# A quarter of every third round's first group is fetched row by row, into two buffers in turn

## The chip, the cores and the metric

One core of one Trainium2 chip. The metric is the device time of the program in microseconds, lower is better. TensorE is PE, VectorE is DVE, ScalarE is ACT, GpSimd is POOL and SyncE is SP.

## The reference

One layer of a graph network with 12500 nodes and 200000 edges, 128 values each, float32:

```
h = relu(layernorm(x))
msg = relu(concat(h[src], h[dst], edge_attr) @ W1 + b1)      # W1: 384 x 128
aggr = segment_sum(msg, dst)
out = x + layernorm(aggr + h) * gamma + beta
```

The receivers dst are sorted, the senders src are not.

## The kernel before, in words

W1 is cut in three. The kernel first computes two tables in HBM, with one row for each node: table_a = h @ W_a and, a few blocks ahead of its use, table_b = h @ W_b + b1. Then it goes through the edges in groups of 512, which lie as 128 partitions by four quarters. Four groups are a round; there are 98 rounds and 391 groups. For the group u of round i:

- SP loads the edge rows and the receivers' numbers for two groups at once (`pair`), and for each group the 64 rows of table_b that its receivers fall into (`window`). The tiles hold one round. So a window is loaded only when the products of the same place in the round before have read it (s_pre), and a pair only when the transposes and the one-hot of the round before are done with it.
- PE transposes the edges (L756), ACT copies them out of PSUM (L991), DVE builds one-hot columns of the receivers (L1367), and PE multiplies both, edges by W_c and one-hot by the window (L769, L770), into one PSUM bank.
- POOL fetches the senders' rows of table_a with four indirect DMAs of 128 rows each (L613, `step`). Their buffers hold one round too: a step waits until the group one round earlier has been added (s_z).
- DVE adds gathered rows and products (L1387, `add_a`), ACT applies relu (L995), PE sums over equal receivers by a one-hot product (L781), and DVE adds the 64 sums into the aggregate in SBUF (L1408).

In each round one block of 128 nodes is finished and stored as well, and one block of table_b is made.

Two kinds of groups don't have all their rows from POOL. In the last round of each six the fourth group comes whole from a table of early rows, which SP loads with one DMA (`load_early`, L497). And in that same round the last quarter of the first group is fetched by hand: the row numbers lie in SBUF as byte offsets (hand_picks), SP and ACT load them into registers (L363, one TENSOR_LOAD for each batch) and issue one DMA of 512 bytes for each row (L508, L1027). Of the 128 rows SP fetches 64, in eight batches of eight, two in each of rounds 1 to 4 of the six (counted from 0), and ACT 64, in batches of four, one in each group of rounds 1 to 4. The first batch waits until the buffer has been read. DVE then adds three quarters from POOL's rows and the last from hand_rows (L1390, L1394).

Each engine goes through its own program in the order in which it is written: within a round that is the order of its `round_`, and semaphores alone tie the engines together. SP, ACT and POOL have a loop whose body is six rounds, called a turn below. SP's rows stand behind the window of the second and of the fourth group of a round.

Of the kernel before, what the change touches and what calls it, by code (L numbers as in the profile page):

```python
# [31 lines left out]
P = 128  # L32
H = 128
EPS = 1e-5
SUB = 4
# [12 lines left out]
PERIOD = 6  # L48
BATCH = 8
HAND_K = SUB - 1  # L50
ACT_ROWS = 64
# [7 lines left out]
def build(nc, x, src, dst, edge_attr, w1, b1, gamma, beta, out):  # L59
# [30 lines left out]
    assert HANDS * PERIOD == ROUNDS - 2 and EARLY % PERIOD == 0 and SP_ROWS % BATCH == 0  # L90
# [7 lines left out]
    with ctx:  # L98
# [69 lines left out]
        hand_rows = sb("hand_rows", [P, 1, H])  # L168
# [122 lines left out]
        s_hand_rows = [sem("s_hand_rows")]  # L291
# [89 lines left out]
        def _(sp):  # L381
# [71 lines left out]
            with sp.If(crooked < 1):  # L453
# [57 lines left out]
                def round_(i, t=None, par=None, j=None):  # L511
# [10 lines left out]
                def rounds(s):  # L522
                    for j in range(EARLY):
                        n = j // PERIOD
                        round_(s * EARLY + j, s * (EARLY // PERIOD) + n, 0, j % PERIOD)
# [10 lines left out]
                with sp.Fori(1, EARLY_GROUPS) as s:  # L536
                    rounds(s)
                round_(ROUNDS - 2)
# [31 lines left out]
        def _(pool):  # L570
# [35 lines left out]
            with pool.If(crooked < 1):  # L606
# [10 lines left out]

                def rounds(s):

                    for n in range(EARLY // PERIOD):  # L620
# [3 lines left out]
                        for u in range(UNROLL if n < EARLY // PERIOD - 1 else UNROLL - 1):  # L624
                            step(s * EARLY + (n + 1) * PERIOD - 1, u, HAND_K if u == 0 else SUB)

                for i in range(EARLY):
                    hand = i % PERIOD == PERIOD - 1
                    for u in range(UNROLL if i < EARLY - 1 else UNROLL - 1):
                        step(i, u, HAND_K if hand and u == 0 else SUB)  # L630
# [242 lines left out]
        def _(act):  # L873
# [111 lines left out]
            with act.If(crooked < 1):  # L985
# [33 lines left out]
                def fetch(t, par, slot):  # L1019

                    if slot == UNROLL and past(t, 1):
                        act.wait_ge(s_z, ((t - 1) * PERIOD + PERIOD - 1) * UNROLL + 1)
                        act.sem_inc(s_gate_act, 1)
                    first = SP_ROWS + sum(ACT_SLOTS[:slot])
                    numbers = numbers_of(mybir.EngineType.Activation, t, first, ACT_SLOTS[slot])
                    for n in range(ACT_SLOTS[slot]):
                        act.dma_start(hand_row(first + n, par), row_at(numbers[n])).then_inc(s_hand_rows[par], 16)  # L1027

                def round_(i, groups=UNROLL, early=False, early_before=False, t=None, par=None, j=None):
                    last = groups < UNROLL  # L1030
                    for u in range(groups):
                        if not (last and u == groups - 1):
                            columns(*after(i, u, 1))
                        if t is not None and j * UNROLL + u < len(ACT_SLOTS) and ACT_SLOTS[j * UNROLL + u]:
                            fetch(t, par, j * UNROLL + u)
# [21 lines left out]

                ACT_SLOTS = [0] * UNROLL + [4] * (ACT_ROWS // 4)
                assert sum(ACT_SLOTS) == ACT_ROWS and len(ACT_SLOTS) < PERIOD * UNROLL

                def rounds(t, early):
                    for j in range(PERIOD):
                        round_(t * PERIOD + j, early=early, early_before=early and (past(t, 1) or j > 0), t=t, par=0, j=j)
# [4 lines left out]
                with act.Fori(1, EARLY_ROWS // PERIOD) as t:  # L1068
                    rounds(t, True)
                t = EARLY_ROWS // PERIOD  # L1070
                for j in range(PERIOD):
                    i = t * PERIOD + j
                    round_(i, early=i < EARLY_ROWS, early_before=i <= EARLY_ROWS, t=t, par=0, j=j)
                with act.Fori(t + 1, HANDS) as t:
                    rounds(t, False)
# [42 lines left out]
        def _(dve):  # L1118
# [232 lines left out]
            with dve.If(crooked < 1):  # L1351
# [21 lines left out]
                def add_a(i, u, turn, loaded, handed):  # L1373
# [6 lines left out]
                    else:  # L1380
                        for k in range(HAND_K if handed is not None else SUB):
                            own = u == UNROLL - 1 or (u == 0 and k == HAND_K)
                            dve.wait_ge(s_a_rows[u][k], (turn if own else i + 1) * 16)  # L1383
# [222 lines left out]
```

## Time and profile before

| | us |
|---|---|
| median of 3 runs | 1952.32 (1952.24 to 1952.49) |
| span of the profiled execution | 1949.5 |
| PE busy | 1548.5 |
| POOL busy | 1463.9 |
| DVE busy | 1256.9 |
| ACT busy | 659.4 |

Shares on the page are of the span. What an engine's sequencer does, such as issuing DMAs, loading registers and waiting for semaphores, doesn't count as busy; it is shown with a q behind the engine's name (SPq, ACTq). SP has no busy time at all on the page, since all that it does is of that kind. "issue" as what ended an idle time means that the engine waited for nothing that the profile shows.

### The profile page before, as it was taken

The page shows a single profiled execution, that of the slowest core. Times are in us where ns is not written, and L with a number is a line of the kernel's source. Part 1 is how long each engine was busy: PE and PEld are TensorE (multiplying, and loading weights), DVE is VectorE, ACT ScalarE, POOL GpSimd, SP SyncE. Part 2 cuts the span into 40 slices and gives each one's busy share as a digit, 9 for nine tenths or more (in the row PEclk, how much of TensorE's full clock was granted, in tenths as well). Part 3 has the DMA queues.
Part 4 walks back from the last instruction along what each step waited for, and adds up shares of the span by engine and source line. Part 5 has one row for each costly group of instructions (what it writes and reads, how often), then busy time and mean ns, then how long its engine had stood idle before and what let it go on. Part 6 is the DMA issues. An engine that isn't in the chain of part 4 may idle for free.

```text
span 1949.5 us, 52908 instructions
## 1 busy us (share of the span) xinstructions
PE 1548.5 (79%) x11881; PEld 1483.7 (76%) x11881; DVE 1256.9 (64%) x3454; ACT 659.4 (34%) x1507; POOL 1463.9 (75%) x1559
## 2 busy tenths in 40 slices
PE   5688788778878787877787788787788888877887
PEld 5678788777777777877777787777777877777786
DVE  7656666667666666666666676666566665656665
ACT  5533333333333333333333333333323232322323
POOL 7777777777777777777777777777777777777776
PEclk9888888989889998998989998999898888888988
DMA  9755656556565655656565565656556565555554
GB/s 261 204 143 144 167 143 166 152 156 166 144 169 145 164 152 155 163 147 169 149 160 153 155 166 144 168 140 168 147 154 163 138 164 148 155 148 153 163 145 106
DMA packets 229468, 306.84 MB, mean 157 GB/s; under 512 B 46461, under 2 KB 141157, under 8 KB 229317
## 3 DMA queue, kind: packets, MB, share of 16 engines
q1 hardware_dynamic: 151858, 192.55, 34.4%
q0 software_dynamic: 49536, 101.55, 21.4%
q10 hardware_dynamic: 27922, 11.43, 2.7%
q14 instruction: 143, 1.16, 0.2%
q8 instruction: 9, 0.15, 0.0%
HBM read 281.72 MB, written 23.64 MB: 157 GB/s over the span
## 4 chain that ended last, share of the span: by engine, by line
issue 22%; DMA 22%; POOL 20%; PE 13%; DVE 10%; DVEq 8%; ACT 2%; ACTq 2%; POOLq 1%; SPq 0%
DMA a_rows<-table_a,picks 20%; POOL a_rows L613 19%; DVEq L1398 5%; DVE onehot_cols L1367 3%; PE ps_pre L769 3%; PE ps_pre L770 3%; PE ps_sum L781 2%; DVE msg L1387 2%; PE ps_edge L756 2%; PE ps_fin L781 1%; DVE aggr L1408 1%; ACTq L1027 1%; DMA table_a<-a_out 1%; DVEq L1383 1%; PE ps_sum L788 1%
## 5 line engine op out<-in xcount | busy, mean ns | idle before, releaser
L613 POOL DMA_INDIRECT a_rows<-table_a,picks x1484 | 1401.8, 945 | 452.4 <-issue 400.3
L769 PE MATMUL ps_pre<-w_c,edge_cols 128*128 128x128 f32 x3128 | 671.5, 300 | 29.5 <-issue 29.2
L770 PE MATMUL ps_pre<-b_win,onehot_cols 128*128 128x128 f32 x3128 | 663.2, 297 | 0.0
L995 ACT ACTIVATE msg<-msg 128x512 f32<-128x512 f32 x390 | 245.7, 630 | 951.9 <-DVE msg L1387 893.1
L769 PEld LDWEIGHTS ps_pre<-w_c,edge_cols 128*128 128x128 f32 x3128 | 537.1, 215 | 38.6 <-issue 37.0
L1387 DVE TENSOR_TENSOR msg<-ps_pre,a_rows 128x512 f32<-128x512 f32 x374 | 257.0, 687 | 433.8 <-DMA a_rows<-table_a,picks 339.4
L770 PEld LDWEIGHTS ps_pre<-b_win,onehot_cols 128*128 128x128 f32 x3128 | 534.7, 214 | 0.0
L1367 DVE SCALAR_TENSOR_TENSOR onehot_cols<-space,base_all,ps_hot 64x512 f32<-64x512 int32 x391 | 438.3, 1121 | 0.6 <-DMA space<-in_dst 0.6
L781 PE MATMUL ps_sum<-onehot,msg 128*128 128x64 f32 x1560 | 214.6, 283 | 105.2 <-ACT e_rows L1013 71.3
L781 PEld LDWEIGHTS ps_sum<-onehot,msg 128*128 128x128 f32 x1560 | 200.5, 201 | 123.4 <-ACT e_rows L1013 82.2
L991 ACT ACTIVATE edge_cols<-ps_edge 128x512 f32<-128x512 f32 x391 | 228.4, 584 | 136.8 <-PE ps_edge L756 115.7
L756 PE MATMUL ps_edge<-ident,edges 128*128 128x128 f32 x1564 | 264.9, 297 | 8.4 <-DMA edges<-in_edge_attr 8.4
L781 PE MATMUL ps_fin<-onehot,msg 128*128 128x64 f32 x1560 | 212.2, 283 | 5.6 <-ACT msg L995 5.6
L781 PEld LDWEIGHTS ps_fin<-onehot,msg 128*128 128x128 f32 x1560 | 205.2, 205 | 7.3 <-DVE aggr L1408 6.9
L756 PEld LDWEIGHTS ps_edge<-ident,edges 128*128 128x128 f32 x1564 | 201.6, 162 | 10.5 <-DMA edges<-in_edge_attr 5.9
L1355 DVE TENSOR_TENSOR onehot<-dst_f,ps_hot 128x256 f32<-128x256 f32 x391 | 161.0, 412 | 41.8 <-issue 34.5
L788 PE MATMUL ps_sum<-ident,e_norm 128*128 128x128 f32 x64 | 24.8, 388 | 120.8 <-DVE e_norm L1426 120.8
L788 PEld LDWEIGHTS ps_sum<-ident,e_norm 128*128 128x128 f32 x64 | 10.0, 156 | 129.8 <-DVE e_norm L1426 129.8
L737 PE MATMUL ps_fin<-ident,staged 128*128 128x128 f32 x97 | 29.6, 305 | 79.3 <-DVE aggr L1408 76.0
L1408 DVE TENSOR_TENSOR aggr<-ps_fin,aggr 128x64 f32 x195 | 43.9, 225 | 72.0 <-issue 44.6
L1408 DVE TENSOR_TENSOR aggr<-ps_sum,aggr 128x64 f32 x196 | 43.8, 224 | 65.8 <-PE ps_sum L781 37.9
L737 PEld LDWEIGHTS ps_fin<-ident,staged 128*128 128x128 f32 x97 | 14.4, 149 | 85.4 <-DVE aggr L1408 83.8
(137 smaller groups left out, 1073.8 us busy)
## 6 DMA issues: line engine op xcount, KB each, us to landing
edges<-in_edge_attr SPq DMA_DIRECT2D x195, 512.0 KB
space<-in_dst SPq DMA_DIRECT2D x195, 256.0 KB
a_rows<-table_a,picks POOLq DMA_INDIRECT x1484
hand_rows<-table_a SPq DMA_DIRECT2D x1024, 0.5 KB
hand_rows<-table_a ACTq DMA_DIRECT2D x1024, 0.5 KB
b_win<-table_b SPq DMA_DIRECT2D x391, 32.0 KB
table_b<-b_rows ACTq DMA_DIRECT2D x96, 64.0 KB
out<-out_rows SPq DMA_DIRECT2D x96, 64.0 KB
```

The costliest lines, as they stand in the source:

```text
L613: pool.indirect_dma_start(a_rows[:, u, k, :], None, table_a[:, :], bass.IndirectOffsetOnAxis(ap=picks[:, u, k:k + 1], axis=0),).then_inc(s ...
L756: mm = pe.transpose(ps_edge[u % 2][:, k * P:(k + 1) * P], edges[:, u, k * H:(k + 1) * H], ident[:, :])
L769: pe.matmul(to, edge_cols[:, u % 2, k * P:(k + 1) * P], w_c[:, :], start=True, stop=False)
L770: mm = pe.matmul(to, onehot_cols[:, u % 2, k * P:(k + 1) * P], b_win[:, u, :], start=False, stop=True)
L781: mm = pe.matmul(ps_sums[u % 2], msg[:, u % 2, k, :], onehot[:, u, k, 0:WIN], start=(k == 0), stop=(k == SUB - 1))
L991: act.activation(edge_cols[:, u % 2, :], ps_edge[u % 2][:, :], ACT.Copy).then_inc(s_edge_cols, 1)
L995: act.activation(msg[:, u % 2, :, :], msg[:, u % 2, :, :], ACT.Relu).then_inc(s_msg, 1)
L1355: dve.tensor_tensor(onehot[:, u, :, 0:WIN], dst_f[:, bass.ds(i * UNROLL + u, 1), :].rearrange("p o k -> p (o k)").unsqueeze(2) .to_broadca ...
L1367: dve.scalar_tensor_tensor(out=onehot_cols[0:WIN, u % 2, :].rearrange("w (k p) -> w k p", k=SUB), in0=dst_win[:, u, :].rearrange("w (p k) ...
L1387: dve.tensor_tensor(msg[:, u % 2, :, :].rearrange("p k f -> p (k f)"), ps_pre[u % 2][:, :], a_rows[:, u, :, :].rearrange("p k f -> p (k f) ...
L1398: return dve.value_load(base_i[0:1, bass.ds(g, 1)], min_val=0, max_val=N - 1)
L1408: dve.tensor_tensor(at, ps_sums[u % 2], at, ALU.add).then_inc(s_added, 1)
```

## The change

A quarter is fetched by hand in every third round in place of every sixth, so 32 times in place of 16. POOL leaves that gather out in the first group of rounds 2 and 5 of each turn. hand_rows has two buffers, used in turn, with a semaphore each. Of the 128 rows SP now fetches 80 and ACT 48. The rows for one use are spread over the three rounds before it: SP has six batches of 13 or 14 rows, behind the windows of the second and the fourth group as before, and ACT has four rows in each of twelve groups. The very first set is fetched in two rounds (SP in four batches of 20, ACT six rows in each group), and the last round of the last turn has no batch. DVE's loops are cut at every third round, and its waits count the gathers of each buffer anew. The core of the diff:

```diff
-PERIOD = 6
-BATCH = 8
+PERIOD = 3
-ACT_ROWS = 64
+ACT_ROWS = 48
...
-        hand_rows = sb("hand_rows", [P, 1, H])
+        hand_rows = sb("hand_rows", [P, 2, H])
...
+        def hand_slots(s, j):
+
+            t = s * 2 + (0 if j < 2 else 1 if j < EARLY - 1 else 2)
+            third = j + 1 if j < 2 else j - 2 if j < EARLY - 1 else 0
+            return t, (j + 1) // PERIOD % 2, third
+
+        def hands_used(t):
+
+            return ((t - 2) * PERIOD + PERIOD - 1) * UNROLL + 1
...
-                def fetch(t, par, batch):
-
-                    if batch == 0 and past(t, 1):
-                        sp.wait_ge(s_z, ((t - 1) * PERIOD + PERIOD - 1) * UNROLL + 1)
+                def fetch(t, par, first, n):
+
+                    if first == 0 and past(t, 2):
+                        sp.wait_ge(s_z, hands_used(t))
                         sp.sem_inc(s_gate_sp, 1)
-                    numbers = numbers_of(mybir.EngineType.SP, t, batch * BATCH, BATCH)
-                    for n in range(BATCH):
-                        sp.dma_start(hand_row(batch * BATCH + n, par), row_at(numbers[n])
-                                     ).then_inc(s_hand_rows[par], 16)
+                    numbers = numbers_of(mybir.EngineType.SP, t, first, n)
+                    for p in range(n):
+                        sp.dma_start(hand_row(first + p, par), row_at(numbers[p])).then_inc(s_hand_rows[par], 16)
...
-                        if t is not None and (j, u) in SP_SLOTS:
-                            fetch(t, par, SP_SLOTS.index((j, u)))
+                        if hands is not None and u % PAIR == 1:
+                            t, par, parts = hands
+                            fetch(t, par, *parts[u // PAIR])
...
-                SP_SLOTS = [(j, u) for j in range(1, PERIOD - 1) for u in (1, 3)]
-                assert len(SP_SLOTS) * BATCH == SP_ROWS
+                def parts(number):
+
+                    ends = [SP_ROWS * n // number for n in range(number + 1)]
+                    return [(first, end - first) for first, end in zip(ends, ends[1:])]
+
+                SP_PARTS, SP_FIRST = parts(2 * PERIOD), parts(4)
...
+                def hand_round(i, groups):
+                    for u in range(groups):
+                        step(i, u, HAND_K if u == 0 else SUB)
+
                 def rounds(s):
 
-                    for n in range(EARLY // PERIOD):
+                    for n in range(2):
                         with pool.Fori(n * PERIOD, (n + 1) * PERIOD - 1) as j:
                             for u in range(UNROLL):
                                 step(s * EARLY + j, u)
-                        for u in range(UNROLL if n < EARLY // PERIOD - 1 else UNROLL - 1):
-                            step(s * EARLY + (n + 1) * PERIOD - 1, u, HAND_K if u == 0 else SUB)
+                        hand_round(s * EARLY + (n + 1) * PERIOD - 1, UNROLL - n)
...
-                ACT_SLOTS = [0] * UNROLL + [4] * (ACT_ROWS // 4)
+                SLOT, FIRST_SLOT = ACT_ROWS // (PERIOD * UNROLL), ACT_ROWS // (2 * UNROLL)
...
-                        dve.wait_ge(s_hand_rows[0], handed * (P * 16))
-                        dve.tensor_tensor(msg[:, u % 2, HAND_K, :], ps_pre[u % 2][:, HAND_K * H:], hand_rows[:, 0, :],
+                        dve.wait_ge(s_hand_rows[par], handed * (P * 16))
+                        dve.tensor_tensor(msg[:, u % 2, HAND_K, :], ps_pre[u % 2][:, HAND_K * H:], hand_rows[:, par, :],
                                           ALU.add).then_inc(s_z, 1)
```

SP's program in the first round of a turn, from the window of the second group to the pair of the third and fourth, before:

```order
L484 REGISTER_ALU
L486 ISA
L486 DMA b_win<-table_b 64x128
L461 ISA
L461 DMA edges<-in_edge_attr 128x2x512
L462 REGISTER_ALU
L462 DMA space<-in_dst 64x1024
```

And now (L495 is the window, L470 and L471 are the pair, L372 is the load of row numbers, L517 the rows):

```order
L493 REGISTER_ALU
L495 ISA
L495 DMA b_win<-table_b 64x128
L372 ISA
L372 TENSOR_LOAD hand_picks
L517 DMA hand_rows<-table_a 1x512 x14
L470 ISA
L470 DMA edges<-in_edge_attr 128x2x512
L471 REGISTER_ALU
L471 DMA space<-in_dst 64x1024
```

A register load and fourteen rows stand between window and pair in a round that had none.

SP's program at the end of a turn, from the window of the fourth group of the sixth round to the jump back, before (L490 is the output store, L497 the load of early rows):

```order
L484 REGISTER_ALU
L486 ISA
L486 DMA b_win<-table_b 64x128
L490 ISA
L490 DMA out<-out_rows 128x128
L495 ISA
L497 ISA
L497 DMA a_rows<-table_early 128x4x128
L536 REGISTER_ALU
L536 COMPARE_AND_BRANCH
```

And now (L499 is the output store, L506 the load of early rows):

```order
L495 ISA
L495 DMA b_win<-table_b 64x128
L372 REGISTER_ALU
L372 TENSOR_LOAD hand_picks
L517 DMA hand_rows<-table_a 1x512 x13
L499 ISA
L499 DMA out<-out_rows 128x128
L504 ISA
L506 ISA
L506 DMA a_rows<-table_early 128x4x128
L554 REGISTER_ALU
L554 COMPARE_AND_BRANCH
```

A batch of thirteen rows stands ahead of the output store, the load of early rows and the jump back.

## Rows read from the trace of the kernel before

**Rows 1.** The page: span, busy time, granted clock by slice, the gather

```profile
span 1949.5 us, 52908 instructions
...
PE 1548.5 (79%) x11881; PEld 1483.7 (76%) x11881; DVE 1256.9 (64%) x3454; ACT 659.4 (34%) x1507; POOL 1463.9 (75%) x1559
...
PEclk9888888989889998998989998999898888888988
...
L613 POOL DMA_INDIRECT a_rows<-table_a,picks x1484 | 1401.8, 945 | 452.4 <-issue 400.3
```

**Rows 2.** Waits of POOL, whole run: line, us in total, times, longest

```profile
POOL a_rows L613 <- issue: 400.3, 1313, 0.3
```

**Rows 3.** L613, 191.8 to 1787.2 us: count, ns min/median/max, first and last

```profile
L613 POOL DMA_INDIRECT a_rows<-table_a,picks x1277: 940/944/1071, 192.0 to 1786.3; - x183
```

**Rows 4.** Waits of DVE, whole run

```profile
DVE msg L1387 <- DMA a_rows<-table_a,picks: 339.4, 154, 5.4
```

**Rows 5.** Waits of SP's queue, 191.8 to 1787.2 us

```profile
SPq L485 <- PE ps_pre L770: 297.5, 89, 8.8
SPq L459 <- DVE onehot_cols L1367: 123.9, 60, 6.7
SPq L490 <- DVE out_rows L1340: 75.5, 30, 5.3
```

**Rows 6.** Timeline of SP: start us, us, line, operation, tiles, count

```profile
1027.92 0.41 SPq L461 DMA_DIRECT2D edges<-in_edge_attr  x1
...
1031.55 2.56 SPq L508 DMA_DIRECT2D hand_rows<-table_a  x8
...
1042.36 2.50 SPq L508 DMA_DIRECT2D hand_rows<-table_a  x8
...
1100.81 0.38 SPq L497 DMA_DIRECT2D a_rows<-table_early  x1
1105.91 0.39 SPq L461 DMA_DIRECT2D edges<-in_edge_attr  x1
```

**Rows 7.** Instructions of L508, whole run

```profile
L508 SPq DMA_DIRECT2D hand_rows<-table_a x1024: 218/225/328, 93.3 to 1878.0; - x171
```

**Rows 8.** Register loads, whole run by tile, then two single ones

```profile
L363 ACTq TENSOR_LOAD <-hand_picks x256: 331/492/696, 110.6 to 1890.0; - x128
L363 SPq TENSOR_LOAD <-hand_picks x128: 525/761/977, 92.6 to 1874.6; - x128
...
L474 SPq TENSOR_LOAD <-base_i x98: 303/569/683, 73.3 to 1914.6; - x98
...
L363 SPq TENSOR_LOAD <-hand_picks x1: 542/542/542, 1014.1 to 1014.1; - x1
...
L363 SPq TENSOR_LOAD <-hand_picks x1: 910/910/910, 1022.8 to 1022.8; - x1
```

**Rows 9.** Timeline of PE: a turned group, products after it, later ones

```profile
1036.46 0.68 PE L756 MATMUL ps_edge<-ident,edges 128*128 128x128 f32 x4
1036.95 0.63 PE L769 MATMUL ps_pre<-w_c,edge_cols 128*128 128x128 f32 x2
...
1041.65 0.39 PE L769 MATMUL ps_pre<-w_c,edge_cols 128*128 128x128 f32 x2
```

**Rows 10.** DMA issue: KB each, median us to landing

```profile
w_c<-in_L_gnn_W SPq DMA_DIRECT2D x1, 64.0 KB, 5.1
```

**Rows 11.** ACT: its longest wait, then four rows in its timeline

```profile
ACT msg L995 <- DVE msg L1387: 893.1, 355, 13.1
...
1090.66 1.45 ACTq L1027 DMA_DIRECT2D hand_rows<-table_a  x4
```

**Rows 12.** Instructions of L1394, whole run

```profile
L1394 DVE TENSOR_TENSOR msg<-ps_pre,hand_rows x16: 268/280/281, 193.1 to 1897.3; 128x128 f32<-128x128 f32 x16
```

**Rows 13.** Waits of SP's queue, 73.3 to 191.8 us

```profile
SPq L485 <- PE ps_pre L770: 30.7, 7, 6.6
SPq L459 <- DVE onehot_cols L1367: 17.8, 5, 8.5
```

More of the change, by code:

```diff
@@ L1017, in store_early, with fetch, round_ @@
                     act.dma_start(table_early[bass.ds(r * P, P), :], e_rows[:, :]).then_inc(s_e_stored, 16)
-                def fetch(t, par, slot):
-                    if slot == UNROLL and past(t, 1):
-                        act.wait_ge(s_z, ((t - 1) * PERIOD + PERIOD - 1) * UNROLL + 1)
+                def fetch(t, par, first, n):
+                    if first == 0 and past(t, 2):
+                        act.wait_ge(s_z, hands_used(t))
                         act.sem_inc(s_gate_act, 1)
[L1024 to L1029, printed above, removed]
+                    numbers = numbers_of(mybir.EngineType.Activation, t, SP_ROWS + first, n)
+                    for p in range(n):
+                        act.dma_start(hand_row(SP_ROWS + first + p, par), row_at(numbers[p])
+                                      ).then_inc(s_hand_rows[par], 16)
+                def round_(i, groups=UNROLL, early=False, early_before=False, hands=None):
                     last = groups < UNROLL
@@ L1033, in round_ @@
                             columns(*after(i, u, 1))
-                        if t is not None and j * UNROLL + u < len(ACT_SLOTS) and ACT_SLOTS[j * UNROLL + u]:
-                            fetch(t, par, j * UNROLL + u)
+                        if hands is not None:
+                            t, par, first, n = hands
+                            fetch(t, par, first + u * n, n)
                         if u == 3 and past(i, 2):
@@ L1067, in _ @@
                 rounds(0, True)
[L1068 to L1075, printed above, removed]
+                with act.Fori(1, EARLY_ROWS // EARLY) as s:
+                    rounds(s, True)
+                half = EARLY_ROWS // EARLY
+                for j in range(EARLY):
+                    i = half * EARLY + j
+                    round_(i, early=i < EARLY_ROWS, early_before=i <= EARLY_ROWS, hands=hands_of(half, j))
+                with act.Fori(half + 1, EARLY_GROUPS - 1) as s:
+                    rounds(s, False)
+                rounds(EARLY_GROUPS - 1, False)
                 round_(ROUNDS - 2)
@@ L1431, in clear, with round_ @@
                     dve.tensor_copy(aggr[:, bass.ds((j + AHEAD) * P, P)], ps_zero.to_broadcast([P, P]))
-                def round_(i, turn, groups=UNROLL, early=False, loaded=None):
+                def round_(i, turn, groups=UNROLL, early=False, loaded=None, handed=None, par=None):
                     last = groups < UNROLL
@@ L1480, in _ @@
                 dve.wait_ge(s_early_raw, EARLY_ROWS * 16)
-                def rounds(s, early):
-                    with dve.Fori(0, EARLY - 1) as j:
-                        round_(s * EARLY + j, s * (EARLY - 1) + j + 1, early=early)
-                    round_(s * EARLY + EARLY - 1, None, early=early, loaded=s + 1)
-                for i in range(3):
-                    round_(i, i + 1, early=True)
-                with dve.Fori(3, EARLY - 1) as i:
-                    round_(i, i + 1, early=True)
@@ L1490, in _, with turns @@
-                round_(EARLY - 1, None, early=True, loaded=1)
-                with dve.Fori(1, EARLY_ROWS // EARLY) as s:
-                    rounds(s, True)
-                half = EARLY_ROWS // EARLY
-                with dve.Fori(EARLY_ROWS - EARLY_REST, EARLY_ROWS) as i:
-                    round_(i, i - half + 1, early=True)
-                with dve.Fori(EARLY_ROWS, half * EARLY + EARLY - 1) as i:
-                    round_(i, i - half + 1)
-                round_(half * EARLY + EARLY - 1, None, loaded=half + 1)
+                def turns(s, j):
+                    return s * (EARLY - 2) + j + (1 if isinstance(j, int) and j < PERIOD else 0), s * (EARLY - 1) + j + 1
@@ new lines, in _ @@
+                for j in range(PERIOD - 1):
+                    round_(j, turns(0, j), early=True)
+                first_hand(0, True)
+                with dve.Fori(PERIOD, EARLY - 1) as j:
+                    round_(j, turns(0, j), early=True)
+                second_hand(0, True)
+                half = EARLY_ROWS // EARLY
+                with dve.Fori(1, half) as s:
+                    rounds(s, True)
+                for j in range(PERIOD - 1):
+                    round_(half * EARLY + j, turns(half, j), early=True)
@@ L1499, in _ @@
+                first_hand(half, True)
+                for j in range(PERIOD, EARLY - 1):
+                    round_(half * EARLY + j, turns(half, j), early=j < EARLY_REST)
+                second_hand(half, False)
                 with dve.Fori(half + 1, EARLY_GROUPS) as s:
                     rounds(s, False)
-                round_(ROUNDS - 2, ROUNDS - 1 - EARLY_GROUPS)
-                round_(ROUNDS - 1, ROUNDS - EARLY_GROUPS, LEFT)
+                round_(ROUNDS - 2, turns(EARLY_GROUPS, 0))
```

61 lines of the change are left out of this document (44 added, 17 removed).

## The prediction

> **What bounds the kernel now.** I read the page first, then who waits for whom, engine by engine, and then single lines. No compute engine is full: the page gives PE 79%, POOL 75%, DVE 64% of the span [rows 1]. But POOL's 75% is the part that the profile counts as busy. Its gather takes 945 ns, 1484 times, and all idle time before gathers is 452.4 us [rows 1], 0.305 us each; in 1313 cases nobody is named for it, and the longest of these is 0.3 us [rows 2]. So a gather costs 945 ns plus 0.3 us whatever the others do, and POOL never stands still for anyone. Take the middle of the run, 191.8 to 1787.2 us, which is 14 turns of the six-round loops (from the start of one turn in SP's stream to that of another): 1277 gathers in 1595.4 us are 1.249 us each [rows 3]. One turn of six rounds takes 1595.4 / 14 = 113.96 us, and 91 gathers of 1.249 us are 113.7 us. The other side of it stands with DVE: its longest wait is for the gathered rows, 339.4 us in 154 waits [rows 4]. POOL bounds the kernel before, and each gather taken from it is worth 1.25 us, for as long as nobody else needs the time.
>
> SP is the next stream to look at, because the change loads it and the page does not show it as an engine at all. In the same 14 turns SP waited 297.5 us for products (to reload a window), 123.9 us for the one-hot (to reload edges) and 75.5 us for output rows: 496.9 us, or 35.5 us a turn [rows 5]. The other 113.96 - 35.5 = 78.5 us of each turn are SP's own instructions, with nothing to wait for. Part of it is the jump back: from the early-table load at 1100.81 to the next edge load at 1105.91 are 5.1 us in which no wait is named [rows 6].
>
> **What the change removes.** Sixteen more groups have their fourth quarter fetched by hand, so POOL has 1484 - 16 = 1468 gathers, 90 a turn instead of 91: 112.4 us a turn. If POOL stayed the bound the kernel would gain 16 x 1.249 = 20.0 us. That is also the most it can gain. POOL's wait for the fetch buffers does not exist (hand rows have their own tile), and two buffers give each set three rounds to be filled and three until it is overwritten, so I cost the gate on the buffer at nothing: the set before last was used three rounds earlier. If that cover failed, the wait would stand on SP's stream, which is priced below.
>
> **What it adds on SP.** Rows a turn go from 64 to 2 x 80 = 160, so 96 more. Eight rows take 2.56 us from first to last, 2.50 at another place [rows 6]; a DMA instruction of 225 ns [rows 7] and the setting up between two of them, 0.32 us all told. 96 x 0.32 = 30.7 us.
>
> Each batch begins with a load of its numbers into registers. Before, 8 loads a turn took 525 to 977 ns, median 761; single ones are 542 ns for the first batch of a round and 910 ns for the second [rows 8]. After there are 12 a turn, each of 13 or 14 numbers instead of 8, and no row shows one of that size. Lower bound: a load costs the same whatever it holds, mean 0.73 us, so 12 x 0.73 - 8 x 0.73 = 2.9 us. Upper bound: in proportion to the numbers, 0.73 x 13.3 / 8 = 1.21 us, 12 x 1.21 - 5.8 = 8.7 us. Between them is the growth from four to eight numbers: SP's loads of four bases take 303 to 683 ns and those of eight 525 to 977 [rows 8], so some 0.055 to 0.08 us a number, which makes 13.3 numbers 0.8 us where the load is quick and 1.3 us where it is slow, 1.06 in the mean: 12 x 1.06 - 5.8 = 6.9 us. I take this one, since both rows it is drawn from are of this engine. The Trainium skill says two things here. DMA: Bandwidth & Descriptors, Latency and other measured facts, puts the floor of a tensor_load at about 600 ns: as a flat price that is 12 x 0.6 = 7.2 us, 1.4 more than now, and on that side the change would come out faster (the second case below). Runtime: NRT & Kernel Launch, Instruction fetch mechanics, has about 200 ns a register, which would be 2.7 us for a load of 13 and a clearly slower kernel, but by that rule eight numbers would take 1.6 us, and the trace has 0.54 and 0.91; the measurement decides, and neither rule is in the sum.
>
> Small things on SP: rounds 0 and 5 of each turn had no rows, and now have them. Loads of bases right after a batch are the slow kind, so two more a turn become slow, 2 x 0.28 = 0.5 us; batch starts and a longer loop body, some 0.6 us (bounds 0 and 1.5).
>
> Sum for SP a turn: 78.5 + 30.7 + 6.9 + 0.5 + 0.6 = 117.2 us, bounds 78.5 + 30.7 + 2.9 = 112.1 and 78.5 + 30.7 + 8.7 + 0.5 + 1.5 = 119.9. POOL would need 112.4, and the turn took 113.96. So the 35.5 us in which SP waited are used up, SP becomes the bound, and a turn takes 3.2 us more than before, not 1.25 less. What queues behind the rows on SP are the edge pairs and the windows: a window can't be loaded before the products of a round earlier have read the old one, so SP can't work ahead by more than about a round, and its lead (the pair issued at 1027.92 is first turned by PE at 1036.46 [rows 6, 9], 8.5 us, of which a landing must be kept, some 4 to 5 us, a little under the 5.1 us that the page gives for a load early in the run [rows 10]) is worth some 4 or 5 us once, not each turn.
>
> At the end of round 5 the batch now stands ahead of the load of early rows. It delays that load by 13 rows and a register load, 5.4 us. DVE needs the tile only after products that the window just before has released, and SP then jumps back and loads edges that PE turns ahead of those products, 5 us later still; so the early rows aren't the last to come. Nothing for it, and at worst 16 x 2 = 32 us if they are.
>
> **On ACT and DVE.** ACT's rows go from 64 to 96 a turn: 8 more batches of 0.49 us for the load and 1.45 us for four rows [rows 8, 11], 16 us a turn, in rounds 0 and 5, where there were none. ACT waits 893.1 us for DVE's sum [rows 11], and the new batches stand just in that wait, as those in rounds 1 to 4 already do while POOL sets the pace. Nothing, and if half a microsecond showed in each it would be 4 us a turn, still beside SP's slack. DVE's sum falls in two parts in 16 more groups, 280 ns for the second part [rows 12] less what the first part saves, under 3 us in all, beside its 339.4 us of waiting. PE has the same work; its granted clock is 0.8 to 0.9 of full in every slice [rows 1], and I leave that.
>
> **The total.** The profiled execution is 1949.5 us long, the runs' median 1952.3, so 2.8 us lie around the span. 14 turns x 3.2 = +45. The first turn (from 73.3 to 191.8, 118.5 us, of which SP waited 48.5 in its two longest waits [rows 8, 13]) has 123 more rows, 39 us, and 9 us more for loads: it fits, with +2. The last turn (1787.2 to 1896.9) took 109.7 us and has no batch in its last round, so SP has room again: -3. The lead that is given up once: -4. Sum: 1952.3 + 45 + 2 - 3 - 4 = 1992.3. I say 1992.
>
> **Rivals.** (1) Loads don't grow with what they hold: SP needs 112.1 to 113.3 us a turn, just at POOL's 112.4, and the kernel gains 1.25 to 0.7 us a turn: 1932 to 1942, faster. It decides from a mean load under about 0.8 us (12 x 0.8 - 5.8 = 3.8 us, a turn of 113). For it: there is a large fixed part in each load. Against it: eight take longer than four at both levels [rows 8], and even here every wait of SP must vanish, though it waits for three different engines. (2) In between, SP needs 113.5 to 114.4, a turn as long as now: 1948 to 1956. (3) SP is full and still has to wait at times, since its lead is gone and the landing of an edge pair now stands in the open before PE: pair, landing, turn, products, next window. From window to window that is about 7.7 us of issuing, 1.5 us for the pair, 5 us to land and 3 to 4 us on PE, some 17 to 18 us, against 19.5 us for SP's own round; with PE at the lower clock, where two products take 0.63 us in place of 0.39 [rows 9], it comes near. At 2 to 4 us a turn: 2025 to 2055. For it: 35.5 us of waits came from this loop. (4) That the change doesn't do what it says: the order of instructions has the batches where the text puts them, so no.
>
> **The chances.** SP full by itself 0.64, rival 3 0.11, rival 2 0.08, rival 1 0.17. Slower by over 0.2% (about what a measurement can tell from no change): 0.64 + 0.11 = 0.75; same 0.08; faster 0.17. The range: 112.1 a turn gives 1932, 119.9 gives 1952.3 + 14 x 5.9 - 5 = 2030. I leave out the best end and most of rival 3, so 1941 to 2028; the likeliest case alone has 1970 to 2024.
>
> **What would show it.** SP's waits for products, one-hot and output rows fall from 496.9 us to under 60 in the middle turns. POOL's gathers remain 945 ns, but the idle time before some of them is now a wait for DVE's sum, 4 to 5 us a turn. DVE waits for products or windows, no longer for gathered rows. Loads of 13 or 14 numbers take about 0.8 and 1.3 us. A turn takes 117 us. I am wrong if POOL's gathers still follow each other by 1.25 us, if the loads take 0.54 and 0.91, or if rows cost other than 0.32 us.

## The result, and the profile after

| | before | after |
|---|---|---|
| median, us | 1952.37 (1952.24 to 1952.49) | 2247.12 (2245.63 to 2249.88) |
| ratio | | 1.151, 95% interval 1.150 to 1.153 |
| span of the profiled execution | 1949.5 | 2243.8 |
| granted PE clock, mean | 0.899 | 0.851 |

The forecast was slower, 1992 us, range 1941 to 2028. The direction came true, the size not: 295 us lost and not 40.

The first question is whether POOL or SP sets the pace now. From the page after, against [rows 1]:

```profile
PE 1613.6 (72%) x11881; PEld 1555.3 (69%) x11881; DVE 1270.1 (57%) x3470; ACT 671.4 (30%) x1507; POOL 1448.1 (65%) x1543
...
SPq 68%; issue 19%; PE 5%; POOL 3%; DMA 3%; DVE 0%; ACTq 0%; ACT 0%; DVEq 0%; POOLq 0%
SPq L517 27%; SPq L372 19%; SPq L495 8%; SPq L471 4%; SPq L470 4%; POOL aggr L607 3%; SPq L483 2%; DMA edges<-in_edge_attr 2%; SPq L499 2%; PE ps_pre L793 1%; PE ps_pre L794 1%; PE ps_edge L780 1%; POOL a_rows L632 1%; DMA a_rows<-table_a,picks 1%; PE ps_sum L805 1%
...
L632 POOL DMA_INDIRECT a_rows<-table_a,picks x1468 | 1385.9, 944 | 762.3 <-issue 447.0
```

POOL has its 16 gathers fewer, of 944 ns each (945 before), but its idle time before them rose from 452.4 to 762.3 us. The chain that ended last is SP's for 68% of the span: the rows (L517), the loads of their numbers (L372), the windows (L495). PE's granted clock is lower than before, but PE has only 5% of that chain.

Fourteen middle turns lie between 203.0 and 2081.9 us (a turn begins with SP's load of bases in its first round). They take 134.21 us each; before it was 113.96. Asked for waits of SP's queue in that stretch, where [rows 5] had 496.9 us, the profile names none. DVE and PE wait for what SP loads, in the same stretch (who waited for whom; us in total, times, longest):

```profile
DVE onehot_cols L1402 <- DMA space<-in_dst: 366.1, 112, 9.4
```

```profile
PE ps_edge L780 <- DMA edges<-in_edge_attr: 413.2, 130, 10.3
```

So SP is full. Its rows cost what they did, against [rows 7]; its loads don't. First the rows, then all loads of hand_picks by SP, in the middle turns, and then four single ones: the third and the fourth batch of one set, and the first and the second of the next (count: ns min/median/max, first and last start in us):

```profile
L517 SPq DMA_DIRECT2D hand_rows<-table_a x2240: 218/225/316, 209.9 to 2080.1; - x187
```

```profile
L372 SPq TENSOR_LOAD <-hand_picks x168: 994/2905/3442, 206.9 to 2072.9; - x168
...
L372 SPq TENSOR_LOAD <-hand_picks x1: 2977/2977/2977, 1010.4 to 1010.4; - x1
...
L372 SPq TENSOR_LOAD <-hand_picks x1: 1393/1393/1393, 1021.1 to 1021.1; - x1
...
L372 SPq TENSOR_LOAD <-hand_picks x1: 1012/1012/1012, 1054.9 to 1054.9; - x1
...
L372 SPq TENSOR_LOAD <-hand_picks x1: 3145/3145/3145, 1063.8 to 1063.8; - x1
```

Loads of 13 or 14 numbers take either 1.0 to 1.4 us or 2.7 to 3.4, while [rows 8] had 0.53 to 0.98 for eight. The load at 1054.9 is the first batch of a set and starts at number 0; the one at 1063.8 has as many numbers and starts at 13. The fourth batch of a set, from number 40 (here at 1021.1), is the other quick one. 0 and 40 are multiples of four; 13, 26, 53 and 66 are not. The loads of a turn sum to 29.4 us. The four loads of the very first set point the same way: they hold 20 numbers each, start at 0, 20, 40 and 60, and take 1.2 to 1.65 us.

### The profile page after: what moved, and what is told of

Its sections match the earlier page's. It is cut to its first block, busy times and chain, and to the rows that moved or that the text cites. A ratio compares the mean times of both kernels' runs of the same rounds, so it can differ in the third digit from the quotient of the medians.

```text
span 2243.8 us, 57022 instructions
## 1 busy us (share of the span) xinstructions
PE 1613.6 (72%) x11881; PEld 1555.3 (69%) x11881; DVE 1270.1 (57%) x3470; ACT 671.4 (30%) x1507; POOL 1448.1 (65%) x1543
## 4 chain that ended last, share of the span: by engine, by line
SPq 68%; issue 19%; PE 5%; POOL 3%; DMA 3%; DVE 0%; ACTq 0%; ACT 0%; DVEq 0%; POOLq 0%
SPq L517 27%; SPq L372 19%; SPq L495 8%; SPq L471 4%; SPq L470 4%; POOL aggr L607 3%; SPq L483 2%; DMA edges<-in_edge_attr 2%; SPq L499 2%; PE ps_pre L793 1%; PE ps_pre L794 1%; PE ps_edge L780 1%; POOL a_rows L632 1%; DMA a_rows<-table_a,picks 1%; PE ps_sum L805 1%
## 5 line engine op out<-in xcount | busy, mean ns | idle before, releaser
L632 POOL DMA_INDIRECT a_rows<-table_a,picks x1468 | 1385.9, 944 | 762.3 <-issue 447.0
L793 PE MATMUL ps_pre<-w_c,edge_cols 128*128 128x128 f32 x3128 | 704.6, 313 | 10.6 <-issue 9.3
L794 PE MATMUL ps_pre<-b_win,onehot_cols 128*128 128x128 f32 x3128 | 697.1, 310 | 0.0
L780 PE MATMUL ps_edge<-ident,edges 128*128 128x128 f32 x1564 | 286.2, 313 | 453.2 <-DMA edges<-in_edge_attr 452.6
L793 PEld LDWEIGHTS ps_pre<-w_c,edge_cols 128*128 128x128 f32 x3128 | 572.9, 228 | 13.3 <-issue 11.9
L794 PEld LDWEIGHTS ps_pre<-b_win,onehot_cols 128*128 128x128 f32 x3128 | 568.8, 227 | 0.0
L805 PE MATMUL ps_sum<-onehot,msg 128*128 128x64 f32 x1560 | 230.7, 297 | 81.5 <-ACT e_rows L1037 60.0
L805 PEld LDWEIGHTS ps_sum<-onehot,msg 128*128 128x128 f32 x1560 | 218.3, 216 | 98.8 <-ACT e_rows L1037 70.9
L607 POOL DMA_INDIRECT aggr<-in_x,early_picks x64 | 60.6, 947 | 22.4 <-issue 18.9
L997 ACT ACTIVATE o_dev<-o_moments,eps 128x1 f32<-128x1 f32 x96 | 28.3, 294 | 155.2 <-issue 154.2
L1227 DVE CAST picks<-src_f 128x4 int32 (+1 forms) x391 | 70.6, 181 | 0.0
L812 PE MATMUL ps_sum<-ident,e_norm 128*128 128x128 f32 x64 | 21.2, 331 | 48.4 <-DVE e_norm L1461 47.7
```

Source lines behind the costliest of these rows:

```text
L632: pool.indirect_dma_start(a_rows[:, u, k, :], None, table_a[:, :], bass.IndirectOffsetOnAxis(ap=picks[:, u, k:k + 1], axis=0),).then_inc(s ...
L780: mm = pe.transpose(ps_edge[u % 2][:, k * P:(k + 1) * P], edges[:, u, k * H:(k + 1) * H], ident[:, :])
L793: pe.matmul(to, edge_cols[:, u % 2, k * P:(k + 1) * P], w_c[:, :], start=True, stop=False)
L794: mm = pe.matmul(to, onehot_cols[:, u % 2, k * P:(k + 1) * P], b_win[:, u, :], start=False, stop=True)
L805: mm = pe.matmul(ps_sums[u % 2], msg[:, u % 2, k, :], onehot[:, u, k, 0:WIN], start=(k == 0), stop=(k == SUB - 1))
```

## The experiments

In the table "turn" is the mean of the fourteen middle turns, "waits" SP's named waits in them, and "own" the difference: SP's instructions with nothing to wait for. POOL's 90 gathers are 112.4 us a turn. Each ratio is taken against runs of the kernel before made beside it, whose medians were 1951.1 to 1954.9 us. Names such as 64 and 48 give SP's rows and ACT's rows of a set.

| kernel | us | ratio to before, interval | turn | waits | own |
|---|---|---|---|---|---|
| before | 1952.4 | | 114.0 | 35.5 | 78.5 |
| after | 2247.1 | 1.151, 1.150 to 1.153 | 134.2 | 0 | 134.2 |
| starts by four | 2013.1 | 1.031, 1.030 to 1.033 | 118.4 | 1.0 | 117.4 |
| padded | 2050.7 | 1.050, 1.049 to 1.052 | 121.1 | 0.7 | 120.4 |
| no loads | 1933.2 | 0.991, 0.989 to 0.992 | 112.4 | 12.1 | 100.3 |
| before, shifted | 1951.0 | 1.000, 0.999 to 1.001 | 114.0 | 27.3 | 86.7 |
| 64 and 64 | 1989.7 | 1.020, 1.017 to 1.023 | 116.6 | 11.5 | 105.1 |
| 72 and 56 | 1951.1 | 1.000, 0.999 to 1.001 | 113.9 | 2.4 | 111.5 |
| 64 and 48 | 1933.6 | 0.991, 0.990 to 0.993 | 112.3 | 7.1 | 105.2 |
| 68 and 60 | 1945.5 | 0.997, 0.995 to 0.998 | 113.6 | 4.8 | 108.8 |
| 72 and 56, merged | 1934.4 | 0.992, 0.990 to 0.993 | 112.4 | 3.7 | 108.7 |
| 80 and 48, merged | 1979.9 | 1.013, 1.012 to 1.015 | 116.0 | 1.5 | 114.5 |

**Loads by themselves, first try.** 96 loads at the end of SP's program, their results unused.

```diff
+                for n in LOAD_SIZES:
+                    for first in LOAD_STARTS:
+                        numbers_of(mybir.EngineType.SP, 0, first, n)
```

> The kernel before, with 96 register loads added at the very end of SP's program, ahead of its last two waits: sizes 1, 2, 4, 8, 12, 13, 14 and 16 numbers, each from twelve starts (0, 1, 2, 3, 4, 8, 16, 13, 26, 40, 53, 66). Their numbers aren't used. Theory A (alignment): a load that starts at a multiple of four numbers (16 bytes) takes 0.3 to 1.0 us, growing by some 0.05 us a number; one that starts elsewhere takes about 0.2 us for each number, so 13 numbers from 13, 26, 53 and 66 take 2.6 to 2.9 us and from 0 and 40 at most 1.0 us. Theory B (count): the start makes no difference, and what costs is a size above eight or one that is no multiple of four: 13 and 14 take 2.6 us or more from every start, 12 and 16 do not. Theory C (neighbours): the slow loads of the changed kernel come from the row DMAs and other traffic around them; alone all sizes stay under 1.2 us. The time is longer than before by what the loads take beyond the wait for the last stores, under 150 us; it tells nothing else.

1954.9 us, and the trace has no load more than before (128 of hand_picks): what nobody uses was left out of the built program. It tells nothing of the theories.

**Starts by four.**

```diff
-                SP_PARTS, SP_FIRST = parts(2 * PERIOD), parts(4)
+                SP_PARTS, SP_FIRST = [(0, 12), (12, 12), (24, 16), (40, 12), (52, 12), (64, 16)], parts(4)
```

> The changed kernel, with SP's six batches of 12, 12, 16, 12, 12 and 16 rows in place of 13 or 14, so that each starts at a multiple of four numbers; as many rows and loads. Theory A: the twelve loads of a turn take 0.8 to 1.5 us each, some 13 us a turn in place of 29.3; SP stays full, the turn falls from 134.3 to 117 to 119 us and the time to 1985 to 2020. Theory B: batches of twelve and sixteen aren't slow either if the fault is a size that is no multiple of four, with the same time; if it is a size above eight, the loads stay near 2.9 us and the time near 2247. Theory C: no change, 2247.

2013.1 us, from 2247.1 with as many rows and loads. The loads:

```profile
L372 SPq TENSOR_LOAD <-hand_picks x190: 752/1136/1652, 76.3 to 1936.9; - x190
```

Theory A, and its turn of 117 to 119 us. Theory C (neighbours) falls; B in its form "a size above eight" falls too. That twelve and sixteen are multiples of four leaves the other form of B.

**Padded.** The batches stay at 13 and 14 rows; each one's numbers get a place of their own.

```diff
+            for m in range(6):
+                a, z = SP_ROWS * m // 6, SP_ROWS * (m + 1) // 6
+                dve.tensor_scalar(hand_picks[:, P + 16 * m:P + 16 * m + z - a], hand_ids[:, a:z, HAND_K],
+                                  float(ROW_BYTES), None, ALU.mult)
...
-                    numbers = numbers_of(mybir.EngineType.SP, t, first, n)
+                    at = first if (first, n) in SP_FIRST else P + 16 * [p[0] for p in SP_PARTS].index(first)
+                    numbers = numbers_of(mybir.EngineType.SP, t, at, n)
```

> The changed kernel with its batches of 13 and 14 rows as they are, but the numbers of each batch copied to a place of its own in hand_picks that starts at a multiple of sixteen numbers (six small DVE copies more, once). Theory A: loads of 13 and 14 take 1.0 us, or 1.4 behind another batch, some 14.5 us a turn in place of 29.3, a turn of 119 us, 2000 to 2025 in all. Theory B (size): no change, 2247. Theory C: no change, 2247.

2050.7 us, 26 over the upper end. The loads took 15.4 us a turn where 14.5 had been worked out, and 0.7 us of waits a turn, which the expectation had left out, stand on top of a full SP:

```profile
L372 SPq TENSOR_LOAD <-hand_picks x190: 981/1330/1693, 77.0 to 1977.4; - x190
```

The same sizes at aligned starts take 1.3 us in place of 2.9. So the start decides nearly all, and a size that is no multiple of four costs some 0.2 us more.

**No loads.** SP's rows come from fixed addresses.

```diff
-                    numbers = numbers_of(mybir.EngineType.SP, t, first, n)
+                    numbers = [(first + p) * ROW_BYTES for p in range(n)]
```

> The changed kernel without SP's register loads: SP fetches rows of fixed addresses, as many and in the same places (the rows it fetches are not those of the senders; ACT's are). If SP's own instructions are the bound, 134.3 - 29.3 = 105 us a turn, or a little less since an address needs no register, are below POOL's 112.4, and the kernel is bound by POOL as before: 1930 to 1940, the full 20 us gained. If instead the 512-byte DMAs themselves, their queue or their landings hold up the pairs and windows, the time stays above 2100.

1933.2 us: the whole worth of the sixteen gathers, 19 of 20 us. The 160 small DMAs a turn hold up nothing; what they cost is SP's time to issue them. (Here they read the same 80 rows again and again. Further down, kernels that fetch the senders' rows, 128 and 144 a turn on SP, reach the same time.) "Own" fell by more than the loads' 29.4 us, to 100.3: a fixed address needs no register, and the 160 moves of 29 ns that stand ahead of the DMAs in the changed kernel, 4.6 us a turn, are gone from the trace.

**Loads by themselves, used.**

```diff
+                for n in LOAD_SIZES:
+                    for first in LOAD_STARTS:
+                        numbers = numbers_of(mybir.EngineType.SP, 0, first, n)
+                        for m in range(n):
+                            ...
+                            sp.dma_start(hand_row(extra % P, 0), row_at(numbers[m])).then_inc(s_more_rows, 16)
+                            extra += 1
```

> The kernel before, with 56 register loads added at the end of SP's program, each followed by one 512-byte row DMA for every number that it loaded, so that the loads can't be dropped as unused: sizes 1, 4, 6, 8, 12, 13 and 16, each from starts 0, 1, 2, 4, 8, 13, 26 and 40. The rows go to a buffer that nobody reads any more. Theory A (alignment): from 0, 4, 8 and 40 a load takes 0.3 to 0.6 us for 4 numbers, 0.9 to 1.4 for 8 to 16; from 1, 2, 13 and 26 about 0.2 us for each number, 0.9 for 4, 1.8 for 8, 2.9 for 13, 3.5 for 16. Theory B (size): no difference between starts. The difference of 13 from 12 at the same start tells whether a rest that is no multiple of four costs extra: 0.2 us more under A.

The loads, by number of values and start, in ns:

```
        start   0      1      2      4      8     13     26     40
 1 number     280    487    484    506    506    499    502    507
 4            529   1136   1124    570    564   1131   1132    564
 6           1005   1528   1527    984    978   1558   1521    985
 8            796   1928   1925    787    783   1835   1921    789
12           1010   2732   2726   1005   1008   2727   2727   1008
13           1243   2928   2928   1237   1234   2923   2928   1230
16           1238   3532   3528   1242   1232   3531   3527   1232
```

Two pairs of them as the trace has them, for 8 and 13 numbers; the quick one starts at 4 and 8, the slow one at 2 and 13:

```profile
L366 SPq TENSOR_LOAD <-hand_picks x1: 787/787/787, 2015.5 to 2015.5; - x1
...
L366 SPq TENSOR_LOAD <-hand_picks x1: 1925/1925/1925, 2010.9 to 2010.9; - x1
...
L366 SPq TENSOR_LOAD <-hand_picks x1: 1234/1234/1234, 2108.0 to 2108.0; - x1
...
L366 SPq TENSOR_LOAD <-hand_picks x1: 2923/2923/2923, 2113.9 to 2113.9; - x1
```

Off a multiple of four, four numbers and more take 0.33 us and 0.2 us for each number. On it, 0.056 us a number in whole fours, and more for a rest: six take 0.99, more than eight. A single number takes 0.5 us from either kind of start; the 280 ns are the first load of all, with no row DMAs ahead of it. The rest is as theory A has it. The time of this run, 2198 us, is that of the added rows at its end and tells nothing else.

**Before, with shifted borders.** It asks whether slow loads hurt as such, or only where SP has no room.

```diff
-                    numbers = numbers_of(mybir.EngineType.SP, t, batch * BATCH, BATCH)
+                    first = batch * BATCH - (2 if batch else 0)
+                    size = BATCH + (2 if batch == 7 else -2 if batch == 0 else 0)
+                    numbers = numbers_of(mybir.EngineType.SP, t, first, size)
```

> The kernel before, with the borders of SP's batches moved by two: 6, then six times 8, then 10 rows, so that seven of eight loads a turn start two past a multiple of four. As many rows and loads. Theory A: those loads take 1.7 to 2.5 us in place of 0.54 and 0.91, 8 to 11 us more a turn on SP, which has 35.5 us of waiting: the loads get slow, SP's waits fall to about 25 us a turn and the time stays within 0.2% of 1952. If slow loads cost in themselves, by holding the pairs and windows late, it is slower by 5 us or more.

```profile
L363 SPq TENSOR_LOAD <-hand_picks x128: 733/1858/2535, 92.1 to 1874.8; - x128
```

Loads of 1.86 us in place of 0.76, 8.2 us more a turn of SP's own time, its waits down from 35.5 to 27.3, and the time equal to 0.1%. The waits were room, and these 8.2 us of it could be used up at no cost.

**64 and 64.** With starts right, how many rows can SP take?

```diff
-ACT_ROWS = 48
+ACT_ROWS = 64
+SP_SIZES, SP_FIRST_SIZES = [12, 8, 12, 12, 8, 12], [16, 16, 16, 16]
+ACT_SIZES, ACT_FIRST_SIZES = [4, 4, 8, 4, 4, 8, 4, 4, 8, 4, 4, 8], [8, 8, 8, 8, 8, 8, 8, 8]
```

> The changed kernel with SP fetching 64 rows in batches of 12, 8, 12, 12, 8, 12 and ACT 64 in 4, 4, 8 repeated; all batches start at a multiple of four numbers. SP's own instructions: 117.6 us a turn in the run with starts by four, less 32 rows of 0.32 us and a little less for loads, 106 to 107, under POOL's 112.4. ACT has eight groups a turn with eight rows, 1.5 us longer there. If SP's instruction time alone was the bound, POOL is it again and the time is 1930 to 1940. If the long ACT batches delay relu and so the sums, 1945 to 1970.

Both miss: 1989.7 us. SP's own time is 105.1, a little under the 106 to 107 worked out, and it waits 11.5 us a turn; POOL waits too, for up to 7.3 us. In the chain that ended last, ACT's queue stands where SP's was, and the timeline of ACT shows how (start, us, engine, line, operation; what ended the idle time before it in brackets):

```profile
PE 32%; issue 18%; ACTq 18%; POOL 8%; DMA 7%; DVE 6%; SPq 4%; ACT 3%; DVEq 3%; POOLq 0%
```

```profile
812.45 0.58 ACT L1016 ACTIVATE edge_cols<-ps_edge 128x512 f32<-128x512 f32 x1
812.95 2.94 ACTq L1051 DMA_DIRECT2D hand_rows<-table_a  x8
816.02 0.28 ACT L1038 ACTIVATE e_rows<-ps_sum 128x128 f32<-128x128 f32 x1 [3.00 <-issue]
816.20 0.62 ACT L1020 ACTIVATE msg<-msg 128x512 f32<-128x512 f32 x1
```

In each of the first 64 rounds ACT also copies a block for the early table out of PSUM, first as columns and then as rows, in the fourth and in the second group, each behind that group's batch. Above, the copy of early rows and then relu stand behind eight rows for 3.00 us. PE waits 103.1 us for those rows and 105.9 for the early columns in this run; with fours alone (64 and 48, below) it is 74.8 and 47.7. Turns with early rows (the first eleven) take 119.3 us on SP. In the later ones ACT has as many rows in the same batches, and POOL's gathers follow each other by 1.249 us again, 360 steps in 449.7 us (window 1400 to 1850 us), so neither ACT's rows nor their batches of eight hold anything up there:

```profile
L633 POOL DMA_INDIRECT a_rows<-table_a,picks x361: 940/944/1057, 1399.7 to 1849.4; - x181
```

I had cost ACT's batches at nothing, and batches of eight ahead of early rows and columns are not.

**72 and 56.**

```diff
+ACT_ROWS = 56
+SP_SIZES, SP_FIRST_SIZES = [12, 12, 12, 12, 12, 12], [20, 16, 20, 16]
+ACT_SIZES, ACT_FIRST_SIZES = [4, 4, 8, 4, 4, 4, 4, 4, 8, 4, 4, 4], [8, 8, 8, 4, 8, 8, 8, 4]
```

> The same with SP fetching 72 rows in six batches of 12, and ACT 56, in 4, 4, 8, 4, 4, 4 repeated. SP's own instructions 117.6 - 16 x 0.32 = 112.5 us a turn, less a little for loads, say 112, as much as POOL's 112.4. Two full streams with waits between them: 1935 to 1960, slower than the run with 64 and 64 if SP's remaining room is what counts, equal to it if a few us of room are enough.

1951.1 us, inside the range and no change to before, with SP nearly full: 111.5 own, 2.4 waiting. Both readings are wrong: it is neither slower than 64 and 64 nor equal to it but faster, although 64 and 64 has more room on SP.

**64 and 48.** As 64 and 64, with all of ACT's batches in the loop four rows; 16 rows of each set aren't fetched.

```diff
+ACT_ROWS = 48
+ACT_SIZES, ACT_FIRST_SIZES = [4, 4, 4, 4, 4, 4, 4, 4, 4, 4, 4, 4], [8, 4, 8, 4, 8, 4, 8, 4]
...
+            dve.memset(hand_rows[:, :, :], 0.0)
...
-                        dve.wait_ge(s_hand_rows[par], handed * (P * 16))
+                        dve.wait_ge(s_hand_rows[par], handed * ((P - 16) * 16))
```

> As the run with 64 rows on SP and 64 on ACT, but ACT fetches 48 in fours, as in the changed kernel, so that 16 rows of each set are not fetched at all and their places keep zeros (the messages of those edges lack the sender's part). It asks why 64 and 64 took 1990 us, 119 to 121 us a turn, with 14 us of waiting on SP. Theory: ACT's batches of eight stand between its copy of the edges and its relu and hold up PE's sums; with fours alone nothing is in POOL's way, SP needs 105 us a turn, and the time is 1930 to 1938. Rival: SP needs more room than its own instruction time leaves, since its lead is short; then it stays at 1960 to 1990.

1933.6 us, with 105.2 us on SP, as in 64 and 64. ACT's part made the difference of 56 us. This run changes two things in it, batches of four and sixteen rows a set fewer. The later turns of 64 and 64 speak against the rows as such, but they have no early copies; in the turns that have them the two are not separated.

**68 and 60.**

```diff
+SP_SIZES, SP_FIRST_SIZES = [12, 12, 12, 12, 12, 8], [20, 16, 16, 16]
+ACT_SIZES, ACT_FIRST_SIZES = [4, 4, 8, 4, 4, 4, 8, 4, 4, 4, 8, 4], [8, 8, 8, 4, 8, 8, 8, 8]
```

> The changed kernel with 68 rows on SP in batches of 12, 12, 12, 12, 12, 8 and 60 on ACT, which has eight rows only in the third group of a round and four elsewhere, where ACT has no copy of early columns or rows behind it. SP needs 111.9 - 8 x 0.32 = 109.3 us a turn. If the long ACT batches cost wherever they stand, 1955 to 1975, between 1951 (two a set) and 1990 (four a set). If they cost only in the second and fourth group, where early rows and columns wait behind them, 1932 to 1948, faster than before.

1945.5 us, inside the second case: against none (64 and 48), three long batches a set, all in the third group, and four more rows on SP cost 12 us. Four long batches a set, one at each of the four places in a round, had cost 56. The number and the place of the long batches changed together, and SP's rows with them, so how the cost is shared is not settled.

**Merged loads.** One load for the two batches of a round, with 72 and 56 rows:

```diff
+                    elif first % 24 == 0:
+                        both = numbers_of(mybir.EngineType.SP, t, first, 2 * n)
+                        kept[:] = both[n:]
+                        numbers = both[:n]
+                    else:
+                        numbers = kept
```

> The changed kernel with 72 rows on SP and 56 on ACT as in the run with that split, but SP loads the 24 numbers of a round at once and issues twelve rows behind the second window and twelve behind the fourth: 6 loads a turn of 24 numbers, 1.7 to 2.0 us each by the growth of aligned loads (0.06 us a number), in place of 12 of some 1.1. SP needs 2 to 3 us a turn less, 109 to 110. If SP is what holds the 72 and 56 split at 114.5 us a turn in its first two thirds, the time falls from 1951 to 1938 to 1948; if ACT's long batches hold it, it stays at 1951.

```profile
L374 SPq TENSOR_LOAD <-hand_picks x97: 1204/1487/1638, 76.7 to 1843.4; - x97
```

1934.4 us, 4 under the expected range and better than both kernels (0.992 of before, 0.861 of after). 24 numbers take 1.49 us, less than I had; SP's own time falls by 2.8 us to 108.7. So SP's instructions held 72 and 56, and not ACT's two long batches a set, which stand in the third group of one round and the first of another. POOL's gathers have no idle time over 0.9 us, near the 0.3 of before the change:

```profile
POOL a_rows L642 <- DVE picks L1234: 47.6, 154, 0.9
```

**80 and 48, merged.** The same on the changed kernel's own split, loads of 28, 24 and 28 numbers from 0, 28 and 52.

```diff
-                SP_PARTS, SP_FIRST = parts(2 * PERIOD), parts(4)
+                SP_PARTS, SP_FIRST = [(0, 14), (14, 14), (28, 12), (40, 12), (52, 14), (66, 14)], parts(4)
...
-                    numbers = numbers_of(mybir.EngineType.SP, t, first, n)
+                    elif SP_PARTS.index((first, n)) % 2 == 0:
+                        both = numbers_of(mybir.EngineType.SP, t, first, 2 * n)
+                        kept[:] = both[n:]
+                        numbers = both[:n]
```

> The changed kernel with its split of 80 and 48 rows and ACT's batches as they are; SP loads the 28, 24 and 28 numbers of a round at once, from starts 0, 28 and 52, and issues half of the rows behind the second window and half behind the fourth. From the two measured SP streams: 117.5 us a turn with twelve aligned loads, and 3.2 us less where merging made six of twelve (111.9 to 108.7), so 114 to 114.5 us a turn, still over POOL's 112.4: SP full, 1955 to 1966 us, slower than before by a little, while 72 and 56 rows with the same loads were faster. If it comes out at 1935 to 1945, SP's instruction time doesn't add up as I have it.

1979.9 us, 14 over the expected range. SP's own time was right, 114.5, but a turn took 116.0: 1.5 us of waits remain on an SP that has no room for them, 21 us over fourteen turns, and the expectation had left them out. What they come from was not tested. Most of SP's waits in those turns are for products; POOL now has gathers that wait up to 4.7 us:

```profile
SPq L494 <- PE ps_pre L803: 16.8, 16, 2.5
```

```profile
POOL a_rows L641 <- DVE picks L1236: 79.5, 130, 4.7
```

## Why the prediction was wrong

The step that failed is the term for the loads: "Between them is the growth from four to eight numbers", 0.8 us where quick and 1.3 where slow, 6.9 us a turn. It measured 29.4 - 5.8 = 23.6 us. The runs showed that the price hangs on the start of the load. The kernel before has starts 0, 8, 16 and so on only, all aligned, so no row of its trace could show the other price; the start had changed with the size, and I didn't name it as a thing that had changed. My upper bound, in proportion to the numbers, was worked out from aligned loads and therefore no bound.

Put in for it, the sum comes out: 117.2 - 6.9 + 23.6 = 133.9 us a turn, and 134.2 was measured. Over fourteen turns the 20.3 us more than before make 284 of the 295 us. And with starts by four the loads are 12.6 us a turn, 6.8 more than before where the term had 6.9: for aligned starts it was right. That kernel takes 2013 us, 21 more than the forecast: its SP needs 117.4 us a turn where 117.2 had been worked out, and 1.0 us of waits a turn come on top, 14 us in all.

Point by point:

- What bounds it before, and that a gather is worth 1.25 us: right. Without SP's loads the gain is 19 us.
- Rows at 0.32 us, 30.7 us a turn: right; the timeline of SP after has 14 rows in 4.43 us (start, us):

```profile
1045.61 4.43 SPq L517 DMA_DIRECT2D hand_rows<-table_a  x14
```

- SP full, all 35.5 us of waits gone: right, to nothing at all. DVE no longer waits for gathered rows, as forecast; it waits for the receivers, and PE for the edges.
- The Trainium skill's rule of some 200 ns a register (Runtime: NRT & Kernel Launch, Instruction fetch mechanics), which I set aside because eight numbers took 0.54 and 0.91 us, is near what an unaligned load costs here: 0.33 us and 0.2 for each number. The page speaks of register loads that the runtime puts in; these are the kernel's own, from SBUF. The trace of before spoke against the rule for aligned starts alone. The Trainium skill's floor of about 600 ns (DMA: Bandwidth & Descriptors, Latency and other measured facts) is no floor here: four bases take as little as 303 ns and eight numbers 525 [rows 8]. As a flat price it fails too, with 0.53 to 0.57 us for four aligned numbers and 1.24 for sixteen.
- Rival 3, waits on top of a full SP: not in the changed kernel, where SP is slow enough that all is there when it comes (0 us). Where SP's own time is over POOL's 112.4 us by less, it exists, smaller than the 2 to 4 us a turn of the rival: 0.7 with 120.4 (padded), 1.0 with 117.4 (starts by four), 1.5 with 114.5 (80 and 48, merged).
- ACT at nothing: right for four rows everywhere, which the run with 64 and 48 shows. With four batches of eight a set (64 and 64) ACT cost 56 us.
- The early rows behind the last batch: nothing found. SP's time alone accounts for the turn.

## What to carry to other kernels

An engine without a busy time can be the next bound. Count its stream for one turn of the loop: its waits are its room, and compare them with what the change adds before looking at anything else. When a size or a count changes, list what changes with it, such as starts and alignment, and treat a price from rows that share the old alignment as unknown for the new one. And shifting work from a full engine to one in the middle of the chain has its own limit: ACT had time for all its rows where nothing urgent stood behind them, but a batch of 3 us held up the copies behind it, for which PE waited. Look at the longest single piece and at what stands behind it, and not at the sum alone.

## What the runs showed that I had not expected

- A register load of four or more numbers from SBUF costs 0.33 us and 0.2 us a number when it starts off a multiple of four numbers (16 bytes), and on it, in whole fours, 0.34 us and 0.056 us a number. 13 numbers: 2.93 against 1.24 us; 16: 3.53 against 1.24.
- The two levels of the loads in the kernel before go by what SP did since its last load. With row DMAs in between, eight numbers take 0.90 to 0.98 us and four bases 0.48 to 0.68; without, 0.53 to 0.62 and 0.30 to 0.33, in all 128 and 98 cases. Why is not shown.
- Six aligned numbers (0.99 us) cost more than eight (0.79), and 24 (1.49 us) little more than 16 (1.24).
- Two thousand more DMAs of 512 bytes cost nothing but the time to issue them: 2560 + 1536 rows in place of 1024 + 1024, and 1933 us without SP's loads.
